# Inverse square roots of a norm-heavy attention and expert layer: Newton steps on VectorE or a power on GpSimd

## The chip, the cores and the metric

The kernel runs on one core of a Trainium2 chip. The metric is the device time of one execution in microseconds (us), lower is better. Engines are called PE (TensorE, matrix products), DVE (VectorE), ACT (ScalarE), POOL (GpSimd) and SP (SyncE, which issues the DMAs).

## What is computed

Input is a batch of 16 sequences of 256 tokens of 128 features, float32. The layer has two halves, both with a residual, both fed by a layer norm without gain:

```python
x = x + attn(layernorm(x))          # 16 heads, keys of 16, values of 64
x = x + ffn(layernorm(x))           # routed experts (16, top 4 in 2 of 4 groups) + a shared one
layernorm(x) = (x - mean) / sqrt(var + 1e-5)
# attn, per head
q, k, v = l2norm(q), l2norm(k), l2norm(v)        # t / max(|t|, 1e-12)
aggr = square(relu(q @ k.T)) @ v
out  = tanh(|aggr|) * aggr / max(|aggr|, 1e-12) * tanh(silu(gates))
y    = concat(out) @ Wout
# ffn
y = sum over chosen experts of weight * (silu(x Wg) * (x Wu)) Wd  + shared expert
```

So per sequence inverse square roots are needed of: 96 head sums of squares per token pair (16 heads of q, k and v, two tokens in each partition row, 96 numbers), 32 squared norms of the aggregate (16 heads, two tokens), and 4 variances (two layer norms, two tokens).

## The kernel before

**Stages.** The batch runs in a software pipeline, one step for each sequence. In step s five stages work on different sequences: L (layer norm and transpose of the input, sequence s + 2), P (projections of q, k, v and gates, their norms and transposes, s + 1), A (scores, squared relu, values, s), O (norm of the aggregate, output projection, residual, second layer norm, s - 1) and F (routing, experts, output, s - 2). Steps run from -2 to 17; steps 4 to 13 are a hardware loop of two steps a turn, the others are written out. All stages are there in steps 2 to 13.

**Slots.** A step has eight slots k = 0 to 7. Stage A takes two heads in each slot: PE makes the scores of the next slot's heads (L435), ACT takes relu out of PSUM (L577), POOL squares it into p (L295), PE multiplies by the values (L464), ACT squares the result (a2, L586), DVE multiplies the result with the gates (L880). Between these, PE works through the table FILL, a list of jobs of the other stages for each slot. Jobs use four PSUM banks in turn: job n can start when job n - 4 has been read out. Slot 1 has gu 0 to 2, slot 2 gu 3 to 7, slot 3 g 0, g 1, gu 8, g 2, rT; slot 4 rB 0 to 3 among others; slot 6 cB 0 to 3; slot 7 y2 0, x2T, xT, y2 1. A gu job is the gate and up product of one pair of experts (L328 to L330; the gate jobs g use the same lines), ACT takes silu (L569), DVE multiplies (L832, `gate_up`) and frees the bank. rT transposes the split head scales rs (L379), rB spreads them (L385), DVE multiplies them into the heads (L840). cT, cB and L850 (`scale_hidden`) do the same for the routing weights and the hidden rows of the experts. x2T (L394) transposes the normalised rows xn2 (L656).

**Order on each engine.** It is written out by hand. Every engine executes its own queue in order and waits on semaphores that count. On DVE every step of a chain of small dependent operations waits for the one before through a semaphore of its own (class `Chain`, `link`).

**The roots.** There are two sets of tiles with m (the argument), y (the root) and t (scratch): `nt` of 128 columns (96 head sums and 32 squares n2, L731 and L914) and `ln` of 4 columns. `seed` (L631, L632) makes the first guess by integer arithmetic on the bits, `newton` (L637 to L639) is one refinement in three instructions; a root takes seed and three refinements, 11 instructions. On DVE the head-norm root stands in slots 1 and 2: seed in slot 1 before gate_up 1 and 2, the refinements in slot 2 before gate_up 3, 4 and 5. Then come gate_up 6, `head_norms` (L744 to L746), gate_up 7, and in slot 3 `head_scales` (L760 to L767, makes rs), `value_scales` (L751 to L755) and gate_up 8. The layer-norm root stands in slot 6 between the four products of `scale_hidden`, and `normed_rows` (L656) begins slot 7.

**POOL's queue** has in each slot the two p products of stage A; in slots 1 and 2 behind them two products each for the low parts of q and k (L305); in slots 4 to 7 behind them one product of the values with their scale (L313). At the start it builds a few constants.

Of the kernel before, what the change touches and what calls it, by code (L numbers as in the profile page):

```python
# [15 lines left out]
RSQRT_MAGIC = 1597463007.0  # L16
# [4 lines left out]
def bass_attn_moe_layer_kernel(nc, tokens, Wqg, Wkv, Wout, gate_kernel, gate_bias,  # L21
# [46 lines left out]
    with ExitStack() as ctx:  # L68
# [17 lines left out]
        ident = sb("ident", [P, P])  # L86
        ones32 = sb("ones32", [P, 2, 32])
# [98 lines left out]
        ch_norms, ch_ln = sem("ch_norms"), sem("ch_ln")  # L186
# [78 lines left out]
        def _(pool):  # L265
# [7 lines left out]

            built(pool.memset(ident[:], 0.0))
# [3 lines left out]
            for part in range(2):  # L278
# [7 lines left out]
                                     pattern=[[-2, 2], [-32, 4], [-1, 2]], channel_multiplier=1))  # L286

            def step(s, q, on, at):
                for k in range(SLOTS):
# [6 lines left out]
                    if "P" in on:  # L296
# [9 lines left out]
                        if k in (4, 5, 6, 7):  # L306
# [7 lines left out]
                                .then_inc(v_normed, 1)  # L314

# [4 lines left out]
        def _(pe):  # L320
            pe.wait_ge(consts_pool, 7)
# [151 lines left out]
        def _(act):  # L473

            act.wait_ge(consts_pool, 2)
# [133 lines left out]
        def _(dve):  # L609
# [18 lines left out]
            def seed(link, tiles):  # L628

                m, y = tiles["m"][:], tiles["y"][:]  # L630
                link(dve.tensor_single_scalar(y.bitcast(I32), m.bitcast(I32), 1, ALU.logical_shift_right))  # L631
                link(dve.tensor_scalar(y.bitcast(I32), y.bitcast(I32), -1.0, RSQRT_MAGIC, ALU.mult, ALU.add))  # L632

            def newton(link, tiles):

                m, y, t = tiles["m"][:], tiles["y"][:], tiles["t"][:]
                link(dve.tensor_tensor(t, m, y, ALU.mult))  # L637
                link(dve.scalar_tensor_tensor(out=t, in0=t, scalar=-0.5, in1=y, op0=ALU.mult, op1=ALU.mult))  # L638
                link(dve.scalar_tensor_tensor(out=y, in0=t, scalar=1.5, in1=y, op0=ALU.add, op1=ALU.mult))  # L639

            RS_OPS = 11
            LN_OPS, NORM_OPS, P_OPS, O_OPS, F_OPS = RS_OPS, RS_OPS, 2, 4, 17

# [24 lines left out]
            dve.wait_ge(consts_pool, 7)  # L668
# [64 lines left out]

            def norms_start(link, P_on, O_on, s):
                if P_on:
                    dve.wait_ge(sums_done, 6 * s + 12)
                if O_on:
                    dve.wait_ge(read["nT"], s)
                seed(link, nt)
# [80 lines left out]
            def step(s, q, on, at):  # L820
# [46 lines left out]
                if P_on or O:  # L867
                    link_norms = Chain(ch_norms, NORM_OPS, s + 1)
                if L_on or O:
                    link_ln = Chain(ch_ln, LN_OPS, s + 2)  # L870
# [25 lines left out]
                for k in range(SLOTS):  # L896
# [7 lines left out]
                    if k == 1:  # L904
# [10 lines left out]
                        if P_on or O:  # L915
                            norms_start(link_norms, P_on, O, s)
# [121 lines left out]
```

## Time and profile before

| | |
|---|---|
| median of 3 runs | 889.2 us (886.67 to 889.55) |
| the profiled execution | 892.35 us |
| its span | 890.6 us |
| mean granted PE clock | 0.944 of full speed |
| busy: PE, DVE, ACT, POOL | 753.3, 687.8, 512.4, 414.9 us |
| DMA | 8.56 MB, all 16 engines busy 3.3% of the span |

The span is from the first to the last instruction of the profiled execution; its own time holds some 1.8 us around it. An engine's busy time is the time in which it executed, waits left out. Each row of a group of instructions has the line, the engine, the operation, the output and input tile with their shapes (partitions x elements), the count, the busy time in us and the mean duration in ns, and behind it the idle time of the engine ahead of them. A row of a timeline has the start and the duration in us, and in square brackets how long the engine sat idle before it and which instruction released it.

### The profile page before, as it was taken

Reading aid. Unit: us, or ns where it says so; the run is one execution under the profiler, and the core shown is the slowest. Engines: PE = TensorE matmul, PEld = TensorE weight load, DVE = VectorE, ACT = ScalarE, POOL = GpSimd, SP = SyncE. Lnnn points to the kernel's source line nnn. Section 1 sums busy time; section 2 is a strip of 40 time slices with the busy share of each in tenths; the row PEclk is TensorE's granted clock in tenths of the full one; section 3 lists DMA queues with packets and bytes.
Section 4 is the critical chain, followed back from the end, with each engine's and each line's share of the span. In section 5 each row is a group of like instructions: output and inputs, shape, how many; then the busy total and the mean of one; then the engine's idle time right before and its main releaser. Section 6 shows DMA issues by size and latency. Waiting matters only on the chain.

```text
span 890.6 us, 17912 instructions
## 1 busy us (share of the span) xinstructions
PE 753.3 (85%) x5440; PEld 586.3 (66%) x5440; DVE 687.8 (77%) x2012; ACT 512.4 (58%) x1112; POOL 414.9 (47%) x395
## 2 busy tenths in 40 slices
PE   3787788889989888988988889898888898887876
PEld 2554557767766766766666677767677676765666
DVE  5767767888787878878788887878778887868654
ACT  4766466566656656666665666665665666643201
POOL 3474555464544645553455555445364645444000
PEclk9889799999999999999999999999999999999877
DMA  7000000000000000000000000000000000000000
GB/s 175 7 1 6 1 7 1 1 14 1 13 1 13 1 8 6 0 12 0 13 0 12 0 0 13 0 12 0 13 0 0 12 0 7 2 7 1 7 7 7
DMA packets 15988, 8.56 MB, mean 10 GB/s; under 512 B 5040, under 2 KB 15664, under 8 KB 15920
## 3 DMA queue, kind: packets, MB, share of 16 engines
q1 hardware_dynamic: 15920, 7.82, 3.3%
q8 instruction: 23, 0.38, 0.2%
q14 instruction: 45, 0.37, 0.1%
HBM read 5.72 MB, written 2.10 MB: 9 GB/s over the span
## 4 chain that ended last, share of the span: by engine, by line
PE 45%; DVE 42%; issue 8%; ACT 4%; POOL 1%; DVEq 1%; POOLq 0%; ACTq 0%
PE ps_a L464 8%; PE ps_f L328 7%; PE ps_f L330 5%; PE ps_f L329 5%; PE ps_f L408 5%; DVE norms_y L639 4%; DVE norms_t L638 4%; DVE ln_t L638 4%; PE ps_s L435 3%; PE ps_f L385 3%; DVE norms_t L637 3%; DVE it L850 3%; DVE it L832 3%; DVE ln_y L639 2%; DVE ln_t L637 2%
## 5 line engine op out<-in xcount | busy, mean ns | idle before, releaser
L295 POOL TENSOR_TENSOR p<-r 128x512 f32<-128x512 f32 x256 | 265.5, 1058 | 390.9 <-ACT r L577 390.9
L577 ACT ACTIVATE r<-ps_s 128x512 f32<-128x512 f32 x256 | 139.0, 599 | 37.2 <-PE ps_s L435 31.7
L464 PE MATMUL ps_a<-p,v 128*64 128x256 f32 x1024 | 147.3, 402 | 5.1 <-POOL p L295 4.5
L544 ACT ACTIVATE qkt<-ps_f 128x512 fp32r<-128x512 f32 x128 | 75.6, 599 | 42.9 <-PE ps_f L362 34.6
L569 ACT ACTIVATE it<-ps_f 128x256 f32<-128x256 f32 x144 | 56.1, 390 | 68.5 <-PE ps_f L330 66.8
L464 PEld LDWEIGHTS ps_a<-p,v 128*64 128x64 f32 x1024 | 64.7, 139 | 45.4 <-issue 6.4
L305 POOL TENSOR_TENSOR qks<-qk,qks 128x512 fp32r<-128x512 f32 x64 | 82.3, 1308 | 13.8 <-DVE qks L720 13.8
L832 DVE TENSOR_TENSOR it<-ps_f,it 128x256 f32<-128x256 f32 x144 | 58.7, 423 | 32.7 <-ACT it L569 25.4
L408 PE MATMUL ps_f<-wdown,it 128*128 128x128 f32 x576 | 75.7, 289 | 8.3 <-DVE it L850 8.3
L880 DVE TENSOR_TENSOR big<-ps_a,wt 128x256 f32<-128x256 f32 x128 | 52.1, 417 | 39.1 <-ACT big L586 27.4
L408 PEld LDWEIGHTS ps_f<-wdown,it 128*128 128x128 f32 x576 | 71.7, 204 | 15.2 <-issue 10.6
L362 PE MATMUL ps_f<-ident,qks 128*128 128x128 f32 x512 | 76.7, 275 | 3.3 <-ACT qkt L544 2.8
L731 DVE TENSOR_REDUCE norms_m<-sq 128x8 f32<-128x512 f32 (+1 forms) x96 | 61.1, 680 | 10.3 <-ACT sq L533 10.3
L435 PE MATMUL ps_s<-qkt 64*128 64x256 f32 x512 | 68.0, 339 | 1.2 <-ACT r L577 0.7
L313 POOL TENSOR_TENSOR v<-v,vs 128x512 f32<-128x512 f32 x64 | 66.6, 1042 | 4.2 <-DVE vs L755 4.2
L840 DVE TENSOR_TENSOR big<-ps_f,big 128x512 f32<-128x512 f32 x64 | 43.6, 691 | 32.3 <-PE ps_f L385 32.3
L385 PE MATMUL ps_f<-rt,sel 128*128 128x256 f32 x256 | 62.9, 333 | 5.6 <-DVE it L850 2.4
L328 PE MATMUL ps_f<-x2h,weg_hi 128*128 128x256 f32 x144 | 48.0, 333 | 21.5 <-DVE it L832 21.5
L389 PEld LDWEIGHTS ps_f<-wout,big 128*128 128x128 f32 x512 | 61.0, 199 | 6.9 <-issue 5.8
L328 PE MATMUL ps_f<-xh,wg_hi 128*128 128x256 f32 x128 | 44.6, 348 | 24.1 <-DVE it L832 23.2
L389 PE MATMUL ps_f<-wout,big 128*128 128x128 f32 x512 | 64.1, 286 | 0.9 <-DVE big L840 0.9
L362 PEld LDWEIGHTS ps_f<-ident,qks 128*128 128x128 f32 x512 | 57.7, 141 | 6.3 <-ACT qkt L544 3.7
(152 smaller groups left out, 1732.3 us busy)
## 6 DMA issues: line engine op xcount, KB each, us to landing
x_in<-in_L_attn_tokens SPq DMA_DIRECT2D x16, 128.0 KB, 2.2
out<-o_sb SPq DMA_DIRECT2D x16, 128.0 KB, 1.8
big<-in_L_attn_Wqg SPq DMA_DIRECT2D x1, 640.0 KB, 3.8
big<-in_L_attn_Wkv SPq DMA_DIRECT2D x1, 640.0 KB, 5.1
big<-in_L_ffn_w_gate SPq DMA_DIRECT2D x1, 512.0 KB, 6.8
big<-in_L_ffn_w_up SPq DMA_DIRECT2D x1, 512.0 KB, 4.8
wout<-in_L_attn_Wout SPq DMA_DIRECT2D x1, 512.0 KB, 4.8
wdown<-in_L_ffn_w_down SPq DMA_DIRECT2D x1, 512.0 KB, 5.7
```

Source lines behind the costliest of these rows:

```text
L295: pool.tensor_tensor(p[h % 4][:], r[h % 2][:], r[h % 2][:], ALU.mult).then_inc(probs_done, 1)
L305: pool.tensor_tensor(lo, whole, hi.bitcast(F32), ALU.subtract).then_inc(qk_lo, 1)
L328: pe.matmul(dst, stat[0], mov[0], start=True, stop=False)
L362: last = pe.transpose(ps[:, part * N + t * P:part * N + (t + 1) * P], src, ident[:])
L385: last = pe.matmul(ps[:, c * N:(c + 1) * N], sel[:, 2 * j + c, :], rt[:], start=True, stop=True)
L389: last = pe.matmul(ps[:, 0:D], aw[pb][:, c, tok[j]], wout[:, c, :], start=(c == 0), stop=(c == NP - 1))
L408: last = pe.matmul(ps[:, 0:D], it[:, c, tok[j]], wdown[:, c, :], start=(c == 0), stop=(c == FC - 1))
L435: last = pe.matmul(ps_s[e][:, t * N:(t + 1) * N], qkt[q][rows, k, N + t * P:N + (t + 1) * P], qkt[q][rows, k, 0:N], start=True, stop=True)
L464: last = pe.matmul(ps_a[k % 2][64 * e:64 * e + 64, 0:N], v[q][:, t, h * DV:(h + 1) * DV], p[h % 4][:, t * N:(t + 1) * N], start=(t == 0), ...
L544: act.activation(qkt[pq][:, j, :], ps[:], ACT.Copy).then_inc(read[kind], 1)
L577: act.activation(r[h % 2][:], ps_s[h % 2][:], ACT.Relu).then_inc(relu_done, 1)
L832: dve.tensor_tensor(it[:, c, :], bank[("gu", c)][:, N:2 * N], it[:, c, :], ALU.mult)\
```

## The change

Both Newton roots leave DVE. Each becomes one instruction of POOL, a tensor_tensor with the operation power, whose second operand is a column of -0.5 broadcast over the tile (a new constant, one more memset at the start). The head-norm root stands in POOL's queue at the end of slot 2, behind the two products of L305, and waits for the last head sum and for n2; DVE waits for it (`norms_ready`) in slot 2 behind gate_up 6. The layer-norm root stands at the end of slot 6, behind the value product, and waits for both row statistics; DVE waits for it (`ln_ready`) at the end of slot 6 behind all four products of `scale_hidden`. The copy of n2 out of PSUM becomes a maximum with 1.2e-38. The scratch tiles t stay allocated.

```diff
@@ -13,7 +13,7 @@
 P = 128
 EPS_LN = 1e-5
 INV_EPS = 1e12
-RSQRT_MAGIC = 1597463007.0
+MIN_N2 = 1.2e-38
 SCALE = 2.5
 SENTINEL = -2.0e38
 
@@ -84,6 +84,7 @@
         bias = sb("bias", [P, E])
 
         ident = sb("ident", [P, P])
+        minus_half = sb("minus_half", [P, 1])
         ones32 = sb("ones32", [P, 2, 32])
         pick = sb("pick", [P, H])
         sel = sb("sel", [P, NP, P], F32R)
@@ -183,7 +184,7 @@
         ln2_ready, x2h_ready = sem("ln2_ready"), sem("x2h_ready")
         silu_done, c_ready = sem("silu_done"), sem("c_ready")
         ch_l, ch_p, ch_o, ch_n, ch_f = (sem(f"ch_{k}") for k in "lponf")
-        ch_norms, ch_ln = sem("ch_norms"), sem("ch_ln")
+        norms_ready, ln_ready = sem("norms_ready"), sem("ln_ready")
 
         block = ctx.enter_context(nc.Block())
 
@@ -271,6 +272,7 @@
                 pool.wait_ge(consts_pool, n[0])
 
 
+            built(pool.memset(minus_half[:], -0.5))
             built(pool.memset(ident[:], 0.0))
             built(pool.affine_select(out=ident[:], in_=ident[:], compare_op=ALU.not_equal, fill=1.0, base=0,
                                      pattern=[[-1, P]], channel_multiplier=1))
@@ -285,6 +287,25 @@
             built(pool.affine_select(out=view, in_=view, compare_op=ALU.not_equal, fill=1.0, base=0,
                                      pattern=[[-2, 2], [-32, 4], [-1, 2]], channel_multiplier=1))
 
+            def root(tiles, ready):
+
+                y = tiles["y"][:]
+                pool.tensor_tensor(y, tiles["m"][:], minus_half[:].broadcast_to(y.shape), ALU.pow).then_inc(ready, 1)
+
+            def norm_roots(s, on):
+                if "P" in on:
+                    pool.wait_ge(sums_done, 6 * s + 12)
+                if "O" in on:
+                    pool.wait_ge(read["nT"], s)
+                root(nt, norms_ready)
+
+            def ln_roots(s, on):
+                if "L" in on:
+                    pool.wait_ge(ch_l, 3 * (s + 3))
+                if "O" in on:
+                    pool.wait_ge(ch_n, 3 * s)
+                root(ln, ln_ready)
+
             def step(s, q, on, at):
                 for k in range(SLOTS):
                     if "A" in on:
@@ -312,13 +333,17 @@
                             scale = vs[:, t, half * NP:(half + 1) * NP]
                             pool.tensor_tensor(view, view, broadcast(scale, [P, NP, DV], 2), ALU.mult)\
                                 .then_inc(v_normed, 1)
+                    if k == 2 and on & {"P", "O"}:
+                        norm_roots(s, on)
+                    if k == 6 and on & {"L", "O"}:
+                        ln_roots(s, on)
 
             run_steps(pool, step)
 
 
         @block.tensor
         def _(pe):
-            pe.wait_ge(consts_pool, 7)
+            pe.wait_ge(consts_pool, 8)
             pe.wait_ge(consts_dve, 2)
 
             weights = {"qk": 2, "v": 3, "g": 4, "gu": 6, "lg": 7, "y": 7, "y2": 7}
@@ -472,7 +497,7 @@
         @block.scalar
         def _(act):
 
-            act.wait_ge(consts_pool, 2)
+            act.wait_ge(consts_pool, 3)
             act.activation(it[0:1, 0, 0:1], ident[0:1, 0:1], ACT.Silu)
             act.wait_ge(w_loaded[0], 32)
             gq = big[:, 0:HK + HV].rearrange("p (h c) -> p h c", h=H)
@@ -625,21 +650,7 @@
                 def end(self):
                     assert self.n == self.per, self.n
 
-            def seed(link, tiles):
-
-                m, y = tiles["m"][:], tiles["y"][:]
-                link(dve.tensor_single_scalar(y.bitcast(I32), m.bitcast(I32), 1, ALU.logical_shift_right))
-                link(dve.tensor_scalar(y.bitcast(I32), y.bitcast(I32), -1.0, RSQRT_MAGIC, ALU.mult, ALU.add))
-
-            def newton(link, tiles):
-
-                m, y, t = tiles["m"][:], tiles["y"][:], tiles["t"][:]
-                link(dve.tensor_tensor(t, m, y, ALU.mult))
-                link(dve.scalar_tensor_tensor(out=t, in0=t, scalar=-0.5, in1=y, op0=ALU.mult, op1=ALU.mult))
-                link(dve.scalar_tensor_tensor(out=y, in0=t, scalar=1.5, in1=y, op0=ALU.add, op1=ALU.mult))
-
-            RS_OPS = 11
-            LN_OPS, NORM_OPS, P_OPS, O_OPS, F_OPS = RS_OPS, RS_OPS, 2, 4, 17
+            P_OPS, O_OPS, F_OPS = 2, 4, 17
 
             def row_stats(link, x, st, mv, part):
 
@@ -665,7 +676,7 @@
                 ins.then_inc(consts_dve, 1)
                 dve.wait_ge(consts_dve, n[0])
 
-            dve.wait_ge(consts_pool, 7)
+            dve.wait_ge(consts_pool, 8)
             dve.tensor_copy(sel[:], selraw)
             dve.memset(rt[:].bitcast(F32), 0.0)
             dve.memset(ones32[:], 0.0)
@@ -730,13 +741,6 @@
                     dst, d = ss3[:, t, 2 * H + half * NP:2 * H + (half + 1) * NP], DV
                 dve.tensor_reduce(dst, squares_at(j).rearrange("p (h d) -> p h d", d=d),
                                   AX.X, ALU.add).then_inc(sums_done, 1)
-
-            def norms_start(link, P_on, O_on, s):
-                if P_on:
-                    dve.wait_ge(sums_done, 6 * s + 12)
-                if O_on:
-                    dve.wait_ge(read["nT"], s)
-                seed(link, nt)
 
             def head_norms(link, b, c):
 
@@ -864,10 +868,6 @@
                     link_p = Chain(ch_p, P_OPS, s + 1)
                 if O:
                     link_n = Chain(ch_n, 3, b)
-                if P_on or O:
-                    link_norms = Chain(ch_norms, NORM_OPS, s + 1)
-                if L_on or O:
-                    link_ln = Chain(ch_ln, LN_OPS, s + 2)
 
                 def gated_heads(k):
 
@@ -911,21 +911,19 @@
                             sums(5, s + 1)
                         if O:
                             dve.wait_ge(done["nT"], b + 1)
-                            dve.tensor_copy(n2, bank[("nT", 0)][:, 0:T * H]).then_inc(read["nT"], 1)
-                        if P_on or O:
-                            norms_start(link_norms, P_on, O, s)
+                            dve.tensor_scalar(n2, bank[("nT", 0)][:, 0:T * H], MIN_N2, None, ALU.max).then_inc(read["nT"], 1)
                         if F:
                             gate_up([1, 2])
                     if k == 2:
                         for c in range(3):
-                            if P_on or O:
-                                newton(link_norms, nt)
                             if F:
                                 gate_up([3 + c])
                             if c == 1:
                                 gated_heads(k)
                         if F:
                             gate_up([6])
+                        if P_on or O:
+                            dve.wait_ge(norms_ready, s + 2)
                         if O:
                             head_norms(link_o, b, rq2[pq])
                         if F:
@@ -971,18 +969,10 @@
                             dve.wait_ge(read["y"], 2 * b + 2)
                             row_stats(link_n, x1[pq], st2, mv2, 1)
                             link_n.end()
+                        if F:
+                            scale_hidden([0, 1, 2, 3])
                         if L_on or O:
-                            seed(link_ln, ln)
-                        if F:
-                            scale_hidden([0, 1])
-                        if L_on or O:
-                            newton(link_ln, ln)
-                        if F:
-                            scale_hidden([2, 3])
-                        if L_on or O:
-                            newton(link_ln, ln)
-                            newton(link_ln, ln)
-                            link_ln.end()
+                            dve.wait_ge(ln_ready, s + 3)
                     if k == 7:
 
                         if O:
```

## Rows read from the trace of the kernel before

**Rows 1.** busy time, share of the span and instructions of each engine, page of the profile

```profile
PE 753.3 (85%) x5440; PEld 586.3 (66%) x5440; DVE 687.8 (77%) x2012; ACT 512.4 (58%) x1112; POOL 414.9 (47%) x395
```

**Rows 2.** stages: length, busy PE, PEld, DVE, ACT, POOL (us), PEclk, DMA share, GB/s

```profile
181.00:232.00 51.00, 45.10 (x341) 35.55 (x340) 41.82 (x121) 31.34 (x70) 25.44 (x25) 0.97 0.02 6
...
691.00:742.00 51.00, 45.18 (x341) 35.30 (x340) 41.30 (x122) 31.71 (x69) 25.49 (x25) 0.97 0.02 5
```

**Rows 3.** timeline of PE, 436 to 488 us

```profile
451.07 0.38 PE L328 MATMUL ps_f<-x2h,weg_hi 128*128 128x256 f32 x1 [1.21 <-DVE it L832]
...
456.18 0.39 PE L328 MATMUL ps_f<-xh,wg_hi 128*128 128x256 f32 x1 [1.77 <-DVE it L832]
...
459.68 0.63 PE L379 MATMUL ps_f<-ident,rs 128*32 128x128 f32 x2
...
471.46 0.38 PE L379 MATMUL ps_f<-ident,cs 128*32 128x128 f32 x2 [0.89 <-DVE cs L767]
...
478.11 2.27 PE L408 MATMUL ps_f<-wdown,it 128*128 128x128 f32 x18 [0.48 <-DVE it L850]
481.81 0.41 PE L394 MATMUL ps_f<-ident,xn 128*128 128x128 f32 x2 [1.43 <-DVE xn L656]
```

**Rows 4.** stretches behind stops of PE, columns as in rows 2

```profile
430.70:436.00 5.30, 5.21 (x38) 4.07 (x39) 2.52 (x9) 2.35 (x6) 1.20 (x2) 1.00 0.10 28
...
451.07:455.90 4.83, 3.33 (x24) 2.33 (x24) 4.45 (x9) 2.40 (x5) 2.77 (x3) 1.00 0.00 0
455.90:459.70 3.80, 3.52 (x19) 3.48 (x20) 3.18 (x16) 1.21 (x3) 0.00 (x0) 0.62 0.00 0
```

**Rows 5.** groups by line and shape, DVE

```profile
L638 DVE SCALAR_TENSOR_TENSOR norms_t<-norms_t,norms_y 128x128 f32<-128x128 f32 x54 | 37.4, 692 | 1.9
...
L638 DVE SCALAR_TENSOR_TENSOR ln_t<-ln_t,ln_y 128x4 f32<-128x4 f32 x57 | 32.6, 572 | 2.0
...
L632 DVE TENSOR_SCALAR norms_y<-norms_y 128x128 int32<-128x128 int32 x18 | 18.8, 1042 | 0.6
```

**Rows 6.** line L638: count, then shortest, median and longest in ns

```profile
L638 DVE SCALAR_TENSOR_TENSOR ln_t<-ln_t,ln_y x57: 161/961/1024, 9.0 to 859.2; 128x4 f32<-128x4 f32 x57
L638 DVE SCALAR_TENSOR_TENSOR norms_t<-norms_t,norms_y x54: 291/1010/1015, 25.3 to 839.2; 128x128 f32<-128x128 f32 x54
```

**Rows 7.** groups by line and shape, POOL

```profile
L295 POOL TENSOR_TENSOR p<-r 128x512 f32<-128x512 f32 x256 | 265.5, 1058 | 390.9 <-ACT r L577 390.9
...
L285 POOL TENSOR_SCALAR_AFFINE_SELECT pick<-pick 128x16 f32<-128x16 f32 x1 | 0.2, 248 | 0.1
```

**Rows 8.** timeline of DVE, 440 to 492 us

```profile
444.80 0.18 DVE L914 COPY norms_m<-ps_f 128x32 f32<-128x32 f32 x1
445.08 0.26 DVE L631 TENSOR_SCALAR norms_y<-norms_m 128x128 int32<-128x128 int32 x1
...
455.70 0.76 DVE L832 TENSOR_TENSOR it<-ps_f,it 128x256 f32<-128x256 f32 x2
...
457.87 0.18 DVE L767 TENSOR_TENSOR rs<-nn,split_hi 128x32 f32<-128x32 f32 x1
...
481.06 0.60 DVE L656 TENSOR_SCALAR xn<-x,mv,ln_y 128x128 f32<-128x128 f32 x2
```

**Rows 9.** timeline of POOL, 440 to 492 us

```profile
448.99 2.61 POOL L305 TENSOR_TENSOR qks<-qk,qks 128x512 fp32r<-128x512 f32 x2
...
475.38 1.04 POOL L313 TENSOR_TENSOR v<-v,vs 128x512 f32<-128x512 f32 x1
477.38 2.04 POOL L295 TENSOR_TENSOR p<-r 128x512 f32<-128x512 f32 x2 [0.95 <-ACT r L577]
```

**Rows 10.** timelines of PE at the edges, 0 to 84 and 790 to 891 us

```profile
35.14 0.66 PE L342 MATMUL ps_f<-ident,xn 128*128 128x128 f32 x2 [4.09 <-DVE xn L656]
...
77.74 0.47 PE L342 MATMUL ps_f<-ident,xn 128*128 128x128 f32 x2 [4.84 <-DVE xn L656]
...
806.51 0.38 PE L379 MATMUL ps_f<-ident,rs 128*32 128x128 f32 x2 [1.75 <-DVE rs L767]
```

## The prediction

> **What bounds the kernel now.** I read the page first. PE is busy 85% of the span, DVE 77%, POOL 47% [rows 1]; none is full, so the bound is a chain that passes from one engine to another. A table of stages then shows that eleven steps in a row, from 181 to 742 us, last 51.0 us each with nearly the same busy times; the first and the last of them stand in [rows 2]: in the first PE 45.1, DVE 41.8, ACT 31.3, POOL 25.4. I read one of the eleven closely, 436 to 487 us; the step behind them, without stage L, is as long. What that step lacks on PE, the timeline of PE says [rows 3]. PE stops five times: 1.21 and 1.77 us in slots 2 and 3 for VectorE's gate-up product (L832), 0.89 for the routing split (L767), 0.48 for the scaled hidden rows (L850), 1.43 for the normalised rows (L656). That is 5.78 us. One more item: after the stops of 1.21 and 1.77 us PE's granted clock is 0.62 over the next 3.8 us, where it was 1.00 between the two stops [rows 4]: most of the stretch lies at the lower of its two levels (1.2 of 2.4 GHz). PE was busy 3.52 us in it; 3.52 x 0.38 = 1.3 us. So PE could do this step in 51.0 - 5.8 - 1.3 = 43.9 us.
>
> Why VectorE is late there: the Newton root stands in its queue between the gate-up products. Its multiplies (L638) have a mean of 692 ns at 128x128 and 572 ns at 128x4, one of the integer seeds 1042 ns [rows 5]. The spread matters more than the mean: the same instruction on 128x4 takes 161 ns at least and 961 ns in the middle, on 128x128 291 and 1010 ns [rows 6]. An instruction that is short in itself waits out a GpSimd product, which takes 1058 ns [rows 7]. The gate-up product, with one input in PSUM, does not show this. So most of the root's time is waiting, and it ends with the instructions.
>
> **The change, part by part.** (a) *VectorE loses* 22 instructions a step. In the step shown the head-norm root begins at 445.08 (behind the n2 copy, 444.80) and ends just before 455.7 [rows 8]; inside are four gate-up products and one head product. Without the root, VectorE reads each gate-up bank as soon as ACT's silu is there. The stops of 1.21 and 1.77 us and the 1.3 us of low clock go: 4.28 us a step, if nothing takes their place.
>
> (b) *GpSimd gains* one power on 128x128 (call it X) in slot 2, behind two p products and two rest-of-key products, and with slot 3's p products queued behind it. GpSimd ends those rest products at 451.6 [rows 9] (448.99 + 2.61), so the roots are ready at 451.6 + X. The sums and n2 that the power waits for are there at 445.0, so that wait costs nothing. VectorE waits for the roots behind gate-up 6; queued behind that wait are the head norms, gate-up 7, head scales, value scales, gate-up 8 and the head product of slot 3. PE waits for gate-up 7 (its bank is that of the third gate job) and for the split head scales (rT). From roots to rs took 2.2 us (455.6 to 457.87 [rows 8]), so rs is ready at 453.8 + X. PE came to rT at 459.68 [rows 3]; without the 4.28 us it comes at 455.4. The new stop is X - 1.6 us. The p products of slot 3 end at 451.6 + X + 2.05, before PE asks for them (it asks after rT), so their delay is covered by the same stop; without that cover they would cost PE nothing until X is 2.7 us.
>
> (c) *X itself* is in no row. Lower bound: a product of 512 elements takes 1058 ns [rows 7], so a pass over 128 takes 0.26 us. A power has to do at least what the removed root did, 11 passes; 11 x 0.26 = 2.9 us. As upper end I take thrice that work, 8.7 us, as logarithm, product and exponential are more than one Newton root. I take X = 2.9: the only row-based count of work there is. Then the stop is 1.3 us, like the one of 1.43 us; behind that stop in the step before, 430.7 to 436, the clock held at 1.00 [rows 4]. So the step gains 4.28 - 1.3 = 3.0 us.
> By the Trainium skill (GPSIMD Engine Reference, Performance pitfalls for Q7 kernels) an fp32 dependent chain costs 4 cycles per element and link; with eleven links, an estimate from that page of 4.7 us for X, the gain of the whole would shrink to about 36 us (14 steps at 6.2 - 3.1 - 1.3, and the edges). No row here shows it.
>
> (d) *Layer-norm root.* Gone: 11 instructions between the four products of L850, which then follow PE directly, so the stop of 0.48 goes. The power on 128x4 stands behind slot 6's v product, which ends at 476.4 [rows 9]; GpSimd was idle until 477.38 there. The smallest comparable GpSimd instruction takes 248 ns [rows 7]; at 0.3 us, or 1 us if a power is dear even for four elements, the roots are there by 477.4, against 481.06 now [rows 8]. PE wants the normalised rows at 481.81 - 1.43 - 0.48 = 479.9, so the 1.43 goes too: 1.9 us a step. GpSimd's next p product is late by a few tenths at most, and PE takes it only at the end of slot 7.
>
> (e) *Small edits.* The copy of n2 becomes a maximum with a constant on the same 128x32: nothing (0.18 us before, at 444.80). One more memset at the start: taken at 0.2 us, by the small GpSimd instruction of 248 ns [rows 7]. The 0.89 us stop at the routing split stays: its chain starts with the scaled heads and is not touched. No DMA and no SP instruction moves.
>
> The shared port: while the power reads SBUF, VectorE's instructions with two SBUF inputs would wait it out, as rows 6 show for the products. In that window VectorE has gate-up and head products only, all with a PSUM input, so I count nothing.
>
> **Sum.** Full steps: s = 1 to 14, fourteen, at 3.0 + 1.9 = 4.9 us: 68.6. At the edges PE stops 4.09, 4.84 and 1.75 us for what the roots delay [rows 10]; I take their sum, 10.7 us, for all the other steps together, bounds 0 and 18. Total 79 us. The profiled execution took 892.35 us (span 890.6), 0.35% above the median of 889.2; off the median that leaves 810 us.
>
> **Rivals.**
> 1. *The power is cheap* (X up to 1.6 us). For: the lower bound of 0.26. No new stop; PE is the bound at 44.8 us a step. 14 x 6.2 + 11 = 98: 791 us. Chance 0.20.
> 2. *The power is middling*, 4.5 to 6.5 us, some 20 passes (20 x 0.26 = 5.2). The new stop is 3 to 5 us, and as after the pair of stops in rows 3 and 4 the clock falls again (1.3 us). The gain per step is 6.2 - 3.6 - 1.3 = 1.3 us: about 860 us. Chance 0.15. The Trainium skill's figure for a dependent chain (GPSIMD Engine Reference) leads here.
> 3. *The power is dear* and GpSimd's queue takes the place of VectorE's: at slot 3 PE waits for rT, VectorE for norms_ready, and slot 3's p products stand behind. It decides from X = 6.5 us, where 6.2 = X - 1.6 + 1.3. At 8.7 us each step loses 2.2 us: 14 x 2.2 = 31, 920 us, edges at nothing. For: no row of a power, and eleven passes is a minimum. Against: 6.5 us is 25 passes. Chance 0.20.
> 4. *Another chain steps in*, ACT above all, which stands in its queue at the tanh of the norms while the gate evacuations wait: half the gain, 850 us. ACT is busy 31.3 of 51 us and would have room. Chance 0.05.
> My forecast (X between 1.6 and 4.5) has 0.40.
>
> **Numbers.** A measurement of this kernel tells 0.3%, 2.7 us, from no change. Slower: rival 3, 0.20. Within 0.3%: the narrow strip round X = 6.5 at the end of rival 2, and a part of rival 4, 0.03. The rest is faster, 0.77. Range: rival 1 with edges of 16 us gives 786 as lower end; the upper end leaves out the dearest powers only, 905 us is X = 7.7.
>
> **What would show it.** Duration of the power on 128x128 on POOL (2.9), on 128x4 (under 1). PE's stops in a steady step: the L832 ones gone, one new stop near rT or at the third gate job of X - 1.6 us, none at L656 or y2; the 0.89 still there. Step 46.1 us, granted clock 1.00 in slot 3. DVE busy near 29 us a step. POOL busy 25.4 + X + 0.3. Wrong if the power is over 4.5 us, if PE waits for p (L295) in slot 3, or if the stop at x2T stays.

## The result: the changed kernel takes a third longer

The changed kernel takes 1197.28 us in the median (1196.55 to 1198.02, 4 runs), the kernel before 889.38 us beside it (886.67 to 891.09, 4 runs). The ratio is 1.348, 95% interval 1.343 to 1.353: slower by 308 us, where 79 us less were forecast and 905 us was the upper end.

**The page of the changed kernel**: its span, the busy times and, from part 4, the shares of the chain that ended last.
```profile
span 1194.7 us, 17373 instructions
...
PE 761.1 (64%) x5440; PEld 588.3 (49%) x5440; DVE 531.2 (44%) x1605; ACT 512.3 (43%) x1112; POOL 800.9 (67%) x433
...
POOL 48%; PE 22%; issue 14%; DVE 12%; ACT 2%; POOLq 1%; DVEq 0%; ACTq 0%
POOL norms_y L293 31%; POOL p L316 8%; POOL qks L326 6%; PE ps_a L489 5%; PE ps_f L353 3%; PE ps_f L410 2%; PE ps_f L433 2%; POOL v L334 2%; PE ps_s L460 2%; PE ps_f L354 2%; PE ps_f L355 2%; PE ps_f L387 1%; DVE nn L748 1%; POOL ln_y L293
```

DVE fell from 688 to 531 us, with 407 instructions fewer. POOL rose from 415 to 801 us and holds 48% of the chain that ended last; in the kernel before it held 1%. One instruction alone, L293 on the norm tiles, is 31% of the chain.

The groups of POOL by line and shape, of the changed kernel (count, busy us, mean ns, then idle time ahead):
```profile
L293 POOL TENSOR_TENSOR norms_y<-norms_m,minus_half 128x128 f32<-128x128 f32 x18 | 373.1, 20725 | 7.3 <-DVE norms_m L914 7.3
L316 POOL TENSOR_TENSOR p<-r 128x512 f32<-128x512 f32 x256 | 262.4, 1047 | 325.3 <-ACT r L602 325.0
...
L293 POOL TENSOR_TENSOR ln_y<-ln_m,minus_half 128x4 f32<-128x4 f32 x19 | 19.2, 1009 | 16.5 <-DVE ln_m L663 16.5
```

**The power on 128x128 takes 20.7 us**, the one on 128x4 1.0 us. The difference over 124 columns is 159 ns a column, which leaves some 0.4 us fixed. The p product of 512 columns beside it takes 1047 ns, 2 ns a column: a column of a power costs as much as 78 columns of a product. This is the number that was in no row of before.

One step of the changed kernel, from one transpose of the routing weights to the next (columns as in [rows 2]):
```profile
370.81:438.82 68.01, 45.72 (x340) 35.72 (x341) 32.68 (x100) 31.62 (x69) 46.91 (x26) 0.82 0.02 5
```

68.0 us where there were 51.0. PE is busy 45.7 us in it, as in before; it is not slower in its work, it waits more. Where, its timeline says (PE, changed kernel, all rows with a wait in one step), and beside it the timelines of POOL and DVE around the root of the next step:
```profile
560.01 0.58 PE L353 MATMUL ps_f<-xh,wg_hi 128*128 128x256 f32 x1 [20.67 <-DVE it L836]
...
575.16 0.38 PE L404 MATMUL ps_f<-ident,cs 128*32 128x128 f32 x2 [0.88 <-DVE cs L771]
...
584.56 0.44 PE L367 MATMUL ps_f<-ident,xn 128*128 128x128 f32 x2 [0.76 <-DVE xn L667]
```
```profile
602.29 2.53 POOL L326 TENSOR_TENSOR qks<-qk,qks 128x512 fp32r<-128x512 f32 x2
604.78 20.72 POOL L293 TENSOR_TENSOR norms_y<-norms_m,minus_half 128x128 f32<-128x128 f32 x1
625.47 2.03 POOL L316 TENSOR_TENSOR p<-r 128x512 f32<-128x512 f32 x2
```
```profile
603.60 0.42 DVE L836 TENSOR_TENSOR it<-ps_f,it 128x256 f32<-128x256 f32 x1 [0.28 <-ACT it L594]
625.53 1.02 DVE L748 TENSOR_TENSOR nn<-norms_m,norms_y 128x32 f32<-128x32 f32 x1 [21.51 <-POOL norms_y L293]
626.59 0.96 DVE L749 TENSOR_TENSOR nn<-nn,rq 128x32 f32<-128x32 f32 x1
627.48 0.18 DVE L750 SCALAR_TENSOR_TENSOR bound<-rq,norms_y 128x32 f32<-128x32 f32 x1
627.78 0.42 DVE L836 TENSOR_TENSOR it<-ps_f,it 128x256 f32<-128x256 f32 x1
```

To be read from the top of the POOL rows: the low-part products end at 604.8, the power runs to 625.5, VectorE, done with gate-up 6 at 604.0, waits 21.5 us for it, and PE gets the bank of gate-up 7 at 628.2 after a wait of 20.67 us (its counterparts of before stand in [rows 3]). The five stops of before have become three: 20.67 at the third gate job, 0.88 at the routing split as before, 0.76 at the transposes of the normalised rows. The sum closes: 45.7 + 20.67 + 0.88 + 0.76 = 68.0 us. GpSimd itself is busy 46.9 of these 68.0 us, less than the 51.0 us of a step of before: it is not full, the loss comes from where the power stands on the path. Whether another place in GpSimd's queue would hide it was not tested.

### The profile page after: what moved, and what is told of

The parts are those of the page before. It is cut to its first block, busy times and chain, and to the rows that moved or that the text cites. A ratio compares the mean times of both kernels' runs of the same rounds, so it can differ in the third digit from the quotient of the medians.

```text
span 1194.7 us, 17373 instructions
## 1 busy us (share of the span) xinstructions
PE 761.1 (64%) x5440; PEld 588.3 (49%) x5440; DVE 531.2 (44%) x1605; ACT 512.3 (43%) x1112; POOL 800.9 (67%) x433
## 4 chain that ended last, share of the span: by engine, by line
POOL 48%; PE 22%; issue 14%; DVE 12%; ACT 2%; POOLq 1%; DVEq 0%; ACTq 0%
POOL norms_y L293 31%; POOL p L316 8%; POOL qks L326 6%; PE ps_a L489 5%; PE ps_f L353 3%; PE ps_f L410 2%; PE ps_f L433 2%; POOL v L334 2%; PE ps_s L460 2%; PE ps_f L354 2%; PE ps_f L355 2%; PE ps_f L387 1%; DVE nn L748 1%; POOL ln_y L293 1%; PE ps_f L414 1%
## 5 line engine op out<-in xcount | busy, mean ns | idle before, releaser
L316 POOL TENSOR_TENSOR p<-r 128x512 f32<-128x512 f32 x256 | 262.4, 1047 | 325.3 <-ACT r L602 325.0
L293 POOL TENSOR_TENSOR norms_y<-norms_m,minus_half 128x128 f32<-128x128 f32 x18 | 373.1, 20725 | 7.3 <-DVE norms_m L914 7.3
L353 PE MATMUL ps_f<-xh,wg_hi 128*128 128x256 f32 x128 | 47.8, 374 | 270.6 <-DVE it L836 268.6
L489 PE MATMUL ps_a<-p,v 128*64 128x256 f32 x1024 | 160.3, 430 | 23.9 <-POOL p L316 23.4
L353 PEld LDWEIGHTS ps_f<-xh,wg_hi 128*128 128x128 f32 x128 | 31.9, 249 | 280.8 <-DVE it L836 271.3
L748 DVE TENSOR_TENSOR nn<-norms_m,norms_y 128x32 f32<-128x32 f32 x16 | 15.5, 970 | 339.5 <-POOL norms_y L293 339.5
L617 ACT ACTIVATE nn<-nn 128x32 f32<-128x32 f32 x16 | 3.7, 229 | 325.6 <-DVE nn L749 325.6
L489 PEld LDWEIGHTS ps_a<-p,v 128*64 128x64 f32 x1024 | 69.0, 148 | 68.7 <-issue 33.3
L460 PE MATMUL ps_s<-qkt 64*128 64x256 f32 x512 | 71.1, 354 | 1.1 <-ACT r L602 0.7
L410 PE MATMUL ps_f<-rt,sel 128*128 128x256 f32 x256 | 65.9, 347 | 4.9 <-DVE it L854 1.7
L844 DVE TENSOR_TENSOR big<-ps_f,big 128x512 f32<-128x512 f32 x64 | 43.4, 691 | 52.7 <-PE ps_f L410 52.7
```

Of the source, the lines that this page charges most:

```text
L293: pool.tensor_tensor(y, tiles["m"][:], minus_half[:].broadcast_to(y.shape), ALU.pow).then_inc(ready, 1)
L316: pool.tensor_tensor(p[h % 4][:], r[h % 2][:], r[h % 2][:], ALU.mult).then_inc(probs_done, 1)
L353: pe.matmul(dst, stat[0], mov[0], start=True, stop=False)
L410: last = pe.matmul(ps[:, c * N:(c + 1) * N], sel[:, 2 * j + c, :], rt[:], start=True, stop=True)
L460: last = pe.matmul(ps_s[e][:, t * N:(t + 1) * N], qkt[q][rows, k, N + t * P:N + (t + 1) * P], qkt[q][rows, k, 0:N], start=True, stop=True)
L489: last = pe.matmul(ps_a[k % 2][64 * e:64 * e + 64, 0:N], v[q][:, t, h * DV:(h + 1) * DV], p[h % 4][:, t * N:(t + 1) * N], start=(t == 0), ...
```

## The experiments

Theory A, from here on: the arrangement does what the prediction worked out (which engine waits for what, and when), and the price of the power was off by a factor of seven. Its rivals: the place in GpSimd's queue costs by itself, the two engines' handing over costs, or the power blocks VectorE at their shared port as a product does [rows 6].

**e1_product: the same arrangement with a cheap instruction.**

```diff
-                pool.tensor_tensor(y, tiles["m"][:], minus_half[:].broadcast_to(y.shape), ALU.pow).then_inc(ready, 1)
+                pool.tensor_tensor(y, minus_half[:].broadcast_to(y.shape), minus_half[:].broadcast_to(y.shape), ALU.mult).then_inc(ready, 1)
```

> Both powers of the changed kernel become a product of the constant column with itself, at the same places, with the same waits (the roots are then the constant 0.25, the heads and rows are wrongly scaled). Theory A (the arrangement is sound, only the price of the power is off): the product on 128x128 takes about 0.3 us, no new stop of PE, 785 to 800 us, by rival 1 of the prediction. Theory B (any instruction of GpSimd at that place, with the waits behind it, holds up the chain): 850 us or more.

Measured: 782.49 us, ratio to before 0.881 (0.878 to 0.883). It leaves out the roots (0.25 stands in their place). The head-norm group of POOL, a step, and two of PE's waits:
```profile
L293 POOL TENSOR_TENSOR norms_y<-minus_half 128x128 f32<-128x128 f32 x18 | 7.2, 400 | 7.3 <-DVE norms_m L914 7.3
```
```profile
368.10:412.23 44.13, 42.92 (x341) 34.10 (x342) 31.34 (x100) 31.29 (x69) 25.84 (x26) 1.00 0.02 7
```
```profile
399.88 0.39 PE L353 MATMUL ps_f<-xh,wg_hi 128*128 128x256 f32 x1 [0.32 <-DVE it L836]
...
412.23 0.38 PE L404 MATMUL ps_f<-ident,cs 128*32 128x128 f32 x2 [0.88 <-DVE cs L771]
```

Theory A, and clearly: every wait, semaphore and queue place of the change is there, only the instruction is cheap, and the kernel is 106 us faster than before. The whole difference between 782 and 1197 us is the duration of the power and what follows from it. The run also corrects a term: a step is 44.1 us, and PE's busy time in it is 42.9 us at a granted clock of 1.00, 2.4 us less than the 45.3 in the step of before that the prediction read. The prediction put the low clock at 1.3 us, from one stretch of 3.8 us [rows 4], and the clock had not fully returned behind it, as the row of the kernel before for the next 3.3 us shows:
```profile
459.70:463.00 3.30, 3.30 (x26) 2.22 (x25) 1.46 (x7) 2.33 (x6) 1.55 (x2) 0.92 0.00 0
```

That is another 0.3 us (3.30 x 0.08), 1.6 in all. From above the clock's part is bounded by e2_ln_only below, where PE has a pair of such stops at a clock of 1.00 and is busy 43.4 us: 1.9 us at most. So the low clock cost 1.6 to 1.9 us a step; where the other 0.5 us of busy time comes from no run shows.

**e2_ln_only and e3_norms_only: one root each.** The first gives the head-norm root back to VectorE (the `seed` and `newton` calls in their old places, `norm_roots` gone from GpSimd), the second the layer-norm root.

```diff
 e2_ln_only
-                    if k == 2 and on & {"P", "O"}:
-                        norm_roots(s, on)
...
+                            norms_start(link_norms, P_on, O, s)
...
+                                newton(link_norms, nt)
 e3_norms_only
-                    if k == 6 and on & {"L", "O"}:
-                        ln_roots(s, on)
...
+                            seed(link_ln, ln)
...
+                            newton(link_ln, ln)
```

> Only the layer-norm root is a power on GpSimd; the head-norm root is the Newton chain on VectorE as before. Theory A: the power on 128x4 takes 1.0 us and ends before PE needs the rows; the stops of 0.48 and 1.43 us of a step go (or shrink to 0.7): 14 x 1.2 to 1.9 = 17 to 27 us and a few at the edges, 855 to 870 us. Theory B: no gain or a loss, 889 or more.

> Only the head-norm root is a power on GpSimd; the layer-norm root is the Newton chain on VectorE as before. Theory A: the whole loss of the changed kernel is here, and its layer-norm gain is missing: 1197 + 14 x 1.2 to 1.9, so 1214 to 1224 us. Theory B (both powers cost): under 1197 us.

Measured: e2_ln_only 851.64 us, ratio 0.959 (0.956 to 0.962), beats both kernels; e3_norms_only 1218.37 us, ratio 1.371 (1.368 to 1.375). The layer-norm half is a gain by itself (37 us against before, 21 us within the changed kernel), and the head-norm half carries all the loss. e2's gain is above its expected 20 to 34 us. POOL, DVE and PE of e2 around the layer norm, and one of its steps:
```profile
405.16 1.04 POOL L336 TENSOR_TENSOR v<-v,vs 128x512 f32<-128x512 f32 x1
406.16 1.01 POOL L295 TENSOR_TENSOR ln_y<-ln_m,minus_half 128x4 f32<-128x4 f32 x1
407.20 2.04 POOL L318 TENSOR_TENSOR p<-r 128x512 f32<-128x512 f32 x2
```
```profile
403.64 2.66 DVE L875 TENSOR_TENSOR it<-ps_f,it 128x512 f32<-128x512 f32 x4 [0.66 <-PE ps_f L410]
407.20 2.12 DVE L681 TENSOR_SCALAR xn<-x,mv,ln_y 128x128 f32<-128x128 f32 x2 [0.90 <-POOL ln_y L295]
```
```profile
410.63 0.44 PE L367 MATMUL ps_f<-ident,xn 128*128 128x128 f32 x2 [0.76 <-DVE xn L681]
...
430.51 0.39 PE L353 MATMUL ps_f<-x2h,weg_hi 128*128 128x256 f32 x1 [1.28 <-DVE it L857]
...
435.78 0.38 PE L353 MATMUL ps_f<-xh,wg_hi 128*128 128x256 f32 x1 [1.96 <-DVE it L857]
```
```profile
401.24:449.51 48.27, 43.39 (x341) 34.10 (x342) 38.87 (x111) 31.63 (x69) 26.46 (x25) 1.00 0.02 6
```

The step is 48.3 us. The stop of 0.48 us is gone and the one of 1.43 us is 0.76, 1.15 us less. PE is busy 43.4 instead of 45.3 us, 1.9 us less, at a clock of 1.00 against 0.97, although the two stops at the gate-up and gate jobs are still there and even 0.3 us longer (1.28 and 1.96 us). Together that is the 2.8 us from the 51.1 of the step that the prediction read to 48.3. In one of four steps in a row the clock did fall, to 0.97, and that step took 49.8 us. Why the clock stays up behind the same pair of stops is not settled by these runs. The 0.76 us that remain are a new term, seen in the first two timelines: the p products of slot 7 now follow the power without a gap, and the pair of normalised rows (L681) takes 2.12 us where it took 0.60 [rows 8]. That the products are the cause here is read from these timelines; no run moved them away.

**f2_width24 and f2_width40: how the time follows X.** The power is cut to its first n columns, the other roots are left out and written as 0.25.

```diff
-                pool.tensor_tensor(y, tiles["m"][:], minus_half[:].broadcast_to(y.shape), ALU.pow).then_inc(ready, 1)
+                pool.tensor_tensor(y[:, n:], rest, rest, ALU.mult)
+                pool.tensor_tensor(y[:, 0:n], m[:, 0:n], half, ALU.pow).then_inc(ready, 1)
```

> The changed kernel with a power on the first 24 of the 128 columns, the other 104 roots are left out (a product of the constant column writes 0.25); the layer-norm root is the full power. With 0.37 us and 159 ns a column the power takes 4.2 us, with the product 4.5. Theory A (the arithmetic of the prediction, stop = X - 1.6, with 1.3 us of low clock behind it): 782 + 14 x (2.9 + 1.3 + 0.8), about 850 us. By a straight line through the two ends (782 us at X up to 1.6, 1197 us at 20.7) 846 us.

> As f2_width24 with 40 columns, 6.7 us, with the product 7.1: just beyond the X = 6.5 us from which the prediction has the change decide for slower. Theory A: 782 + 14 x (5.5 + 1.3 + 0.8) = 888 us, no change against before within 1.5%. By the straight line 901 us. If the break-even lies elsewhere, a step of the reasoning other than the price was off too.

Measured: 894.59 us (ratio 1.011, 1.004 to 1.018) with 24 columns and 951.18 us (1.074, 1.067 to 1.081) with 40. Both miss, by 45 and 63 us. The power's duration is right, what follows from it is not. First the rows of 24 columns (group, a step, PE's stop), then those of 40:
```profile
L298 POOL TENSOR_TENSOR norms_y<-norms_m,minus_half 128x24 f32<-128x24 f32 x18 | 74.7, 4152 | 0.0
```
```profile
374.94:426.11 51.17, 45.13 (x340) 35.14 (x341) 32.69 (x100) 31.65 (x69) 30.64 (x27) 0.93 0.02 5
...
411.70:416.40 4.70, 4.67 (x21) 2.88 (x21) 2.46 (x15) 2.30 (x6) 1.16 (x2) 0.51 0.00 0
```
```profile
411.73 0.58 PE L358 MATMUL ps_f<-xh,wg_hi 128*128 128x256 f32 x1 [4.41 <-DVE it L841]
```
```profile
L298 POOL TENSOR_TENSOR norms_y<-norms_m,minus_half 128x40 f32<-128x40 f32 x18 | 121.4, 6744 | 0.0
```
```profile
399.16:453.74 54.58, 45.98 (x340) 35.97 (x341) 32.72 (x100) 31.65 (x69) 33.21 (x27) 0.91 0.02 5
```
```profile
438.52 0.58 PE L358 MATMUL ps_f<-xh,wg_hi 128*128 128x256 f32 x1 [6.97 <-DVE it L841]
```

With the product of the rest, the powers' time in the queue is 0.40 (e1), 4.47, 7.04 and 20.72 us (changed kernel), and PE's stop is 0.32, 4.41, 6.97 and 20.67 us. So **the stop is X less 0.05 to 0.08 us** over the whole range; the prediction had X - 1.6. The slack of 1.6 us that PE was to have is not there. And PE's busy time in a step goes 42.9, 45.1, 46.0, 45.7 us: one long stop costs 2.2 to 3.1 us of lower clock (0.51 over the 4.7 us behind the stop of 4.41 us), not 1.3. With both, a step at X = 4.5 us is 51.2 us, that of before 51.0. Between the two widths the kernel takes 22 us more for each us of X, and the narrower one is 9.6 us above before. By an estimate from these numbers the change decides for slower from X = 4.0 us, not from 6.5.

**g1_products_wait: where the slack went.** In the DVE rows of the changed kernel the two head-norm multiplies take 1.02 and 0.96 us; in before they took 0.18 each. They start with the slot-3 products that follow the power at once.

```diff
                 root(nt, norms_ready)
+                if "O" in on:
+                    pool.wait_ge(n_ready, s)
```

> The changed kernel with one more wait: GpSimd's products of slot 3, which follow the power at once, first wait for VectorE's two head-norm multiplies (n_ready). Theory A (the term that the prediction missed: these products block the two multiplies, 1.02 and 0.96 us instead of 0.18 each): with the wait the multiplies take 0.18 us each, PE's stop falls from 20.67 to about 19.1 us, 1197 - 14 x 1.6 = 1175 us, although the products start 0.4 us later. Theory B (the handing over from engine to engine costs that time): no change or slower, 1197 to 1205 us.

Measured: 1183.77 us, ratio 1.333 (1.325 to 1.342), 13.5 us less than the changed kernel. DVE and PE:
```profile
553.26 0.19 DVE L750 TENSOR_TENSOR nn<-norms_m,norms_y 128x32 f32<-128x32 f32 x1 [21.51 <-POOL norms_y L293]
553.49 0.19 DVE L751 TENSOR_TENSOR nn<-nn,rq 128x32 f32<-128x32 f32 x1
```
```profile
554.38 0.58 PE L355 MATMUL ps_f<-xh,wg_hi 128*128 128x256 f32 x1 [19.06 <-DVE it L838]
...
556.45 0.58 PE L406 MATMUL ps_f<-ident,rs 128*32 128x128 f32 x2 [0.42 <-DVE rs L773]
```

**A wait more, and the kernel is faster.** The multiplies take 0.19 us, and PE's stop is 19.06 us, 1.61 less, which is the slack that was missing. The gain of the whole is smaller than 14 x 1.6 because a stop of 0.42 us appears at rT: the delayed products now stand beside two later instructions of the chain to rs (0.76 and 0.95 us). So the prediction's count of what PE waits for was right, and what was wrong is the 2.2 us from the roots to rs, read in a step of before in which no product stood next to the head norms.

**g2_gate7_first: is it the root or the queue behind it?**

```diff
                         if F:
-                            gate_up([6])
+                            gate_up([6, 7])
                         ...
                         if O:
                             head_norms(link_o, b, rq2[pq])
-                        if F:
-                            gate_up([7])
```

> The changed kernel with gate-up 7 moved ahead of VectorE's wait for the roots (it does not need them). PE's 20.67 us stop at the third gate job goes over to rT, which waits for rs: PE does the third gate job (0.7 us at full clock) before the stop and not behind it. Theory A (the roots themselves are what PE waits for): a stop of 20 us at L404 in slot 3, 14 x 0.7 = 10 us less, 1187 us. Theory B (it was gate-up 7's place in the queue that hurt, the roots have slack): the stop shrinks by several us, under 1150 us.

Measured: 1188.76 us, ratio 1.339 (1.331 to 1.347), 8.5 us less. PE:
```profile
558.97 0.58 PE L404 MATMUL ps_f<-ident,rs 128*32 128x128 f32 x2 [20.53 <-DVE rs L771]
```

Theory A, within 2 us: the stop of 20.5 us only moves on to rT. This order on VectorE does not hide the power, its result is on the path.

**e4_idle_power and f1_power_slot1: a power for which nobody waits.** Both are the kernel before with its Newton roots. e4 adds a power on a constant at the end of slot 2, f1 one in place on a tile of its own at the end of slot 1. The cut shows e4's line; f1's reads and writes the tile `spare`.

```diff
+                    if k == 2 and on & {"P", "O"}:      # f1_power_slot1: k == 1
+                        pool.tensor_tensor(spare_out[:], spare_in[:].broadcast_to([P, P]), minus_half[:].broadcast_to([P, P]), ALU.pow)
```

> The kernel before, untouched in its Newton roots, with one more power of 128x128 in GpSimd's queue at the end of slot 2 of each step; its input is a constant (3.7) and nobody waits for it. If only the wait for the roots costs (the products of slot 3 behind the power are covered): 889 us. If GpSimd's queue costs by itself: the products of slot 3 end at 451.6 + 20.7 + 2.0 = 474.3 in the step shown and PE asks for them at 460.7, 13.6 us later each step, about 1100 us. If the power also holds the shared SBUF port for its whole time, VectorE's Newton multiplies behind its start wait up to 20 us each time (line L638 with single durations of 15 to 20 us), and the time is near the changed kernel's, 1150 to 1200 us. Its duration on a constant input also shows whether the 20.7 us hang on the data.

> The kernel before with one more power on 128x128, in place on a tile of its own, in GpSimd's queue at the end of slot 1, so that VectorE's whole head-norm Newton chain (multiplies with two SBUF inputs) falls into the power's 20.7 us. Theory A (a power takes nothing from VectorE): L638's counterpart on 128x128 has a median near 290 ns; the time is set by the products of slot 2 queued behind the power, PE asks for them some 14 us before they are there: 1100 to 1200 us. Theory B (the power holds the shared read port as a product does): single Newton multiplies of 15 us and more, the gate-up products behind them late by as much, 1200 us or more.

Measured: e4 1156.91 us, ratio 1.302 (1.299 to 1.305); f1 1155.91 us in one run, with before at 885.03. e4's POOL and PE, then f1's POOL and PE, then the counterparts of L638 in e4 and in f1 (count, shortest/median/longest ns):
```profile
522.84 20.76 POOL L319 TENSOR_TENSOR spare_out<-spare_in,minus_half 128x128 f32<-128x128 f32 x1
543.58 4.02 POOL L298 TENSOR_TENSOR p<-r 128x512 f32<-128x512 f32 x4
```
```profile
544.75 2.87 PE L469 MATMUL ps_a<-p,v 128*64 128x256 f32 x8 [15.62 <-POOL p L298]
```
```profile
525.11 20.72 POOL L319 TENSOR_TENSOR spare<-spare,minus_half 128x128 f32<-128x128 f32 x1
```
```profile
546.99 2.87 PE L469 MATMUL ps_a<-p,v 128*64 128x256 f32 x8 [17.38 <-POOL p L298]
```
```profile
L643 DVE SCALAR_TENSOR_TENSOR norms_t<-norms_t,norms_y x54: 291/370/1250, 25.7 to 1104.1; 128x128 f32<-128x128 f32 x54
L643 DVE SCALAR_TENSOR_TENSOR norms_t<-norms_t,norms_y x54: 291/292/295, 25.4 to 1104.6; 128x128 f32<-128x128 f32 x54
```

Three readings. The queue costs by itself: PE stops 15.62 us for p (L469), which stands behind the power, though nobody uses its result. So there are two paths with nearly the same price, roots to PE and p to PE, and the queue alone costs 268 us where the change costs 308. The duration is the same on a constant (20.76 us) and on the sums (20.72). And the power does not block VectorE: in f1 the Newton multiplies, two SBUF inputs each, take 291 to 295 ns, all 54, and all of them lie within the 20.7 us of a power; in e4, where part of them still stand beside products, the longest takes 1.25 us and none the 15 to 20 of a held port. e4 was expected at 1100 us for the queue and at 1150 to 1200 if the port were held; it came to 1157 without a held port, because the stop was 15.6 and not 13.6 us (the chain on VectorE is quicker beside a power than beside products, so PE arrives sooner) and the clock fell behind it (0.57 over the next 4.3 us). The time alone would have spoken for the wrong theory, and the rows decide it.

**f3_two_refinements, g3_low_parts_moved, h1_both_moved: what the Newton chain costs on VectorE.** All three start from e2_ln_only.

```diff
 f3_two_refinements
-                            if P_on or O:
+                            if c > 0 and (P_on or O):
                                 newton(link_norms, nt)
 g3_low_parts_moved
-                        if k in (1, 2):
-                            t = k - 1
+                        if k in (0, 3):
+                            t = k // 3
 h1_both_moved: g3_low_parts_moved and the order of g2_gate7_first
```

> e2_ln_only (layer-norm root a power on GpSimd, 851.6 us) with two Newton refinements in the head-norm root instead of three, so three VectorE instructions fewer in slot 2 (less precise, about 5e-6 relative). Theory A (what counts is an instruction's place behind a GpSimd product, 0.85 us each on average): PE's stops of 1.28 and 1.96 us and part of the low clock go, 14 x 2.5 to 3.5, 803 to 817 us. Theory B (only their own 0.29 us each count): 14 x 0.9, 839 us.

> e2_ln_only (851.6 us) with GpSimd's low-part products (L305 of the kernel before, 2.5 us a pair) in slots 0 and 3 instead of 1 and 2, out of the way of VectorE's head-norm Newton chain; nothing is left out. Theory A (the root is slow because it waits out GpSimd's products, rows 6 of the prediction): the chain of 11 gets 2 to 3 us shorter, PE's stops of 1.28 and 1.96 us shrink and the clock does not fall, 803 to 820 us. Theory B (the number of instructions is what counts): 851 us.

> g3_low_parts_moved (836.5 us) with gate-up 7 ahead of the head norms on VectorE. In g3 PE's stop of 1.76 us at the third gate job stayed, since the low-part products now run in slot 3 and block two head-norm instructions (1.19 and 1.31 us) ahead of gate-up 7. Theory A: with gate-up 7 first that stop goes, and PE finds rs ready or late by at most 1 us at rT: 14 x 0.8 to 1.8 less, 811 to 825 us. Theory B (rT becomes the same stop, as in g2): the gain is the third gate job's 0.7 us at most, 14 x 0.7, 827 us.

Measured: f3 836.83 us (0.946, 0.938 to 0.953), g3 836.51 us (0.941, 0.935 to 0.947), h1 836.92 us (0.944, 0.942 to 0.947). f3 lands on theory B, g3 between its two, h1 on neither, with no gain over g3. DVE and PE of g3, then PE of h1:
```profile
423.40 0.29 DVE L663 SCALAR_TENSOR_TENSOR norms_t<-norms_t,norms_y 128x128 f32<-128x128 f32 x1
423.73 1.07 DVE L664 SCALAR_TENSOR_TENSOR norms_y<-norms_t,norms_y 128x128 f32<-128x128 f32 x1
...
425.80 1.19 DVE L770 TENSOR_TENSOR nn<-nn,rq 128x32 f32<-128x32 f32 x1
426.91 1.31 DVE L771 SCALAR_TENSOR_TENSOR bound<-rq,norms_y 128x32 f32<-128x32 f32 x1
428.34 0.42 DVE L857 TENSOR_TENSOR it<-ps_f,it 128x256 f32<-128x256 f32 x1
```
```profile
425.39 0.38 PE L353 MATMUL ps_f<-xh,wg_hi 128*128 128x256 f32 x1 [0.59 <-DVE it L857]
...
428.82 0.38 PE L353 MATMUL ps_f<-xh,wg_hi 128*128 128x256 f32 x1 [1.76 <-DVE it L857]
```
```profile
424.21 0.38 PE L404 MATMUL ps_f<-ident,rs 128*32 128x128 f32 x2 [1.72 <-DVE rs L792]
```

In g3 the chain of 11 with what lies between takes 8.1 us (416.8 to 424.9) instead of 10.8 in e2 (424.5 to 435.3), and moving GpSimd's products away gives the kernel as much (15 us) as leaving out three instructions of the root. But the second stop stays, 1.76 us: the low parts now stand beside the head norms, and two of these take 1.19 and 1.31 us. The contention was moved, not removed. With gate-up 7 ahead (h1) PE stops 1.72 us at rT instead, and two head norms still take 1.06 and 1.20 us: again the result itself is late, not the queue behind it. These three beat both kernels; g3 and h1 compute all that before computes, f3 with one refinement less.

## Why the prediction was wrong

By its own steps:

- **(c), the price of the power, is the step that failed.** It was taken as 11 passes of a product's rate, 2.9 us, with 8.7 as upper end; it is 20.7 us, 78 passes. The bound from above was no bound: that a power is at most three Newton roots' work was a guess that no row showed, and the range (to 905 us, X = 7.7) rested on it. A price between 0.26 us and unknown should have been carried to where the verdict turns, and the far side given its chance. The estimate from the Trainium skill (GPSIMD Engine Reference, Performance pitfalls for Q7 kernels), 4.7 us for a dependent chain, was nearer and still far too low.
- (a), what VectorE loses, was right: in e1_product the stops of 1.21 and 1.77 us are gone (0.32 left). The clock's part was 1.6 to 1.9 us a step and not 1.3.
- (b), who waits for what, was right (the third gate job and rT, p behind them). The slack of 1.6 us was wrong: products that follow the power at once block the head norms, 1.6 us (shown by g1). The break-even is near 4 us, by the estimate above. The 2.2 us from the roots to rs were also read from the start of the last instruction (457.87); it ends 0.18 us later.
- (b) also held the p products covered by the same stop. True in the changed kernel, but the power in their queue alone costs 268 us (e4).
- (d), the layer norm, was right in kind: 1.0 us for the power, stops from 1.91 to 0.76 us. The rest is by its timeline the same missed term, a product right behind a power; no run isolates it there.
- (e) was right: the stop at the routing split stayed, 0.88 us.
- The rivals: the third (a dear power, GpSimd's queue in VectorE's place) is what happened, with its mechanism and place as told. It had 0.20. Its formula with X = 20.7 gives 14 x 14.2 = 199 us; measured were 308. Of the 17 us a step that were measured 14.2 are the formula's, and the rest is the blocked head norms (1.6), the 0.76 stop and the clock; the edges, which it took at nothing, are the remaining 70 us: the two first and two last steps with a root stop too, by 20.6, 18.9, 19.9 and 16.3 us.
- The first rival (PE becomes the bound, 44.8 us a step, 791 us) was confirmed by e1_product: 44.1 us and 782 us.

## What to carry over

Before work is moved to another engine, run that one instruction there at its real size; a price that no row shows has no upper end, and where the verdict turns on it the forecast is about that price alone. Cut a moved operation by size: the 4-column root was worth moving (0.959), the 128-column one was not. And an instruction in a queue on which others depend costs time even if nobody waits for its result (here a stop of 15.6 us for 20.8 us of duration), and what is released right behind it can block the work that it was to release.

## What the runs showed of the hardware

- A power on GpSimd takes 0.4 us and 159 ns a column of 128 partitions: 1.01 us at 4, 4.15 at 24, 6.74 at 40, 20.7 at 128, there on the sums and on a constant alike.
- VectorE's instructions with two SBUF inputs run at their own speed beside a power (291 to 295 ns, f1), and wait out a product (median 1010 ns, [rows 6]; a product takes 1058 [rows 7]). The Trainium skill (SBUF — State Buffer, Who interferes with whom) lets a VectorE instruction with two SBUF inputs contend with a GpSimd instruction that reads SBUF, and calls the shared port pair an exclusive lock; the products agree with it, the power of f1, which reads its tile in SBUF, does not. What a power does with the port in its 20 us was not tested further.
- Behind a stop of 4.41 us PE's granted clock is 0.51, near its lower level of 1.2 GHz, over the next 4.7 us (f2_width24), and behind the stop of 15.6 us it is 0.57 over 4.3 us (e4). Behind stops of 1.21 and 1.77 us it fell in the kernel before [rows 4]; behind stops of 1.28 and 1.96 us it held at 1.00 in three of four steps of e2_ln_only. What decides is open.
